# Audio tower on one core: tokens, attention and experts in one pass; two steps of the expert round, the emptying of a shared bank and the routing are put elsewhere in the order

## What is computed

```
h = tok(x)            # 3 patch sizes (8, 16, 32; stride half a patch): 127 + 63 + 31 = 221 tokens of 128
                      # each token = patch @ W_i.T + b_i + pos_i + scale_emb_i
h = h + attn(layernorm(h))     # 8 heads of 16, softmax over the 221 tokens, output matrix w_agg
h = h + ffn(layernorm(h))      # "batch" of 1024 tokens: 2 of 8 experts per token,
                               # y = gelu(z @ w1[e]) @ w2[e], added with the router weight
```

## Time and profile before

| what | value |
|---|---|
| runs, median | 309.08 us (306.54 to 309.54) |
| the profiled execution | 307.14 us |
| its span | 305.3 us |
| TensorE busy, share of the span | 269.8 us, 88% |
| VectorE busy | 199.5 us, 65% |
| ScalarE busy | 143.3 us, 47% |
| GpSimd busy | 109.4 us, 36% |
| TensorE's mean granted clock | 0.935 of full speed |

### The profile page before, as it was taken

One profiled execution on the slowest core, in us unless ns is written; L12 is line 12 of the kernel. 1 busy time (PEld: TensorE's weight loads), 2 busy tenths in 40 slices (PEclk: granted clock), 3 DMA queues, 4 the chain that ended last, 5 costly groups with the idle time before them and its releaser, 6 DMA issues.

```text
span 305.3 us, 7681 instructions
## 1 busy us (share of the span) xinstructions
PE 269.8 (88%) x3147; PEld 230.8 (76%) x3147; DVE 199.5 (65%) x440; ACT 143.3 (47%) x220; POOL 109.4 (36%) x172
## 2 busy tenths in 40 slices
PE   8999869889999999999979798998979797998461
PEld 8999859677879797979768696877868696877331
DVE  4786674787888678785745567574756656475654
ACT  4650414533434352525456557564666466565220
POOL 4000220102455555555614264543636272422200
PEclk9999988999999999999979889997999899899755
DMA  7999000394000000000210020111011010001241
GB/s 206 380 381 422 9 1 2 84 344 125 20 10 24 15 22 15 18 24 13 68 29 17 11 54 17 36 34 37 26 34 37 10 52 11 17 26 35 78 136 46
DMA packets 19466, 22.33 MB, mean 73 GB/s; under 512 B 2416, under 2 KB 15448, under 8 KB 19400
## 3 DMA queue, kind: packets, MB, share of 16 engines
q1 hardware_dynamic: 17671, 19.24, 20.1%
q0 software_dynamic: 1760, 2.60, 2.8%
HBM read 17.42 MB, written 5.95 MB: 77 GB/s over the span
## 4 chain that ended last, share of the span: by engine, by line
PE 69%; DVE 12%; issue 6%; ACT 6%; DMA 4%; POOL 1%; SPq 0%; DVEq 0%; POOLq 0%; ACTq 0%
PE e_ps L982 13%; PE s_ps L1065 12%; PE s_ps L982 7%; PE e_ps L1186 7%; DVE nmax L801 7%; PE m_ps L1050 5%; PE m_ps L1173 4%; PE m_ps L1131 4%; PE s_ps L1118 3%; PE e_ps L1173 2%; PE m_ps L1040 2%; PE m_ps L1142 2%; DMA x_raw<-x 2%; DMA y_rows<-y_sb,idx_u 2%; ACT hidT L588 1%
## 5 line engine op out<-in xcount | busy, mean ns | idle before, releaser
L801 DVE TENSOR_REDUCE nmax<-s_ps 128x4 fp32r<-128x884 f32 (+1 forms) x64 | 65.9, 1071 | 24.8 <-PE s_ps L1065 24.8
L573 ACT ACTIVATE probs<-s_ps 128x888 f32<-128x888 f32 (+1 forms) x64 | 54.7, 906 | 57.9 <-PE s_ps L1118 57.9
L473 POOL DMA_INDIRECT y_rows<-y_sb,idx_u x23 | 23.0, 999 | 62.5 <-PE s_ps L1118 40.2
L1131 PE MATMUL m_ps<-probs,v_aug 93*32 93x221 f32 (+1 forms) x512 | 28.8, 366 | 0.7 <-ACT probs L573 0.7
L454 POOL DMA_INDIRECT z_slots<-z,slot_u x20 | 22.6, 1128 | 16.4 <-PE s_ps L1118 11.8
L1050 PE MATMUL m_ps<-zT,wqkv_sb 128*128 128x221 f32 x64 | 17.3, 397 | 11.4 <-ACT h_sb L553 11.4
L426 POOL TENSOR_TENSOR var_eps<-mv,eps_t 128x2 f32<-128x2 f32 x16 | 3.2, 201 | 66.4 <-DVE mv L768 66.2
L1186 PE MATMUL e_ps<-w_now,hidT 128*128 128x128 f32 x184 | 25.3, 290 | 0.0
L786 DVE TENSOR_TENSOR k_lo<-m_ps,k_hi 128x442 fp32r<-128x442 f32 x16 | 9.9, 619 | 23.6 <-ACT k_hi L566 23.6
L1186 PEld LDWEIGHTS e_ps<-w_now,hidT 128*128 128x128 f32 x184 | 23.2, 203 | 1.3 <-issue 1.0
L1065 PE MATMUL s_ps<-k_hi,q_a 32*128 32x222 f32 (+1 forms) x256 | 18.5, 308 | 4.6 <-DVE nmax L801 3.3
(11 more groups left out here) (125 smaller groups left out, 619.6 us busy)
## 6 DMA issues: line engine op xcount, KB each, us to landing
w_raw<-wt SPq DMA_DIRECT2D x6, 512.0 KB, 9.5
x_raw<-x SPq DMA_DIRECT2D x6, 512.0 KB, 9.9
w_sb<-w SPq DMA_DIRECT2D x1, 2048.0 KB, 9.6
z_slots<-z SPq DMA_DIRECT2D x1, 1518.0 KB, 9.5
zs<-z_slots SPq DMA_DIRECT2D x7, 198.0 KB, 2.6
x_raw<-x SPq DMA_DIRECT2D x4, 256.0 KB, 5.1
out<-h SPq DMA_DIRECT2D x11, 64.0 KB
c_sb<-consts SPq DMA_DIRECT2D x1, 599.0 KB, 11.6
```

Source lines behind the costliest of these rows:

```text
L473: g.indirect_dma_start(y_dram, bass.IndirectOffsetOnAxis(ap=idx_u[:, at:at + 1], axis=0), y_sb[:, i, :], None).then_inc(y_out, 16)
L573: s.activation(probs[0:n, blk, 2 * f:2 * f + 2].rearrange("p t u n -> p t (u n)"), s_ps[0:n, 2 * f:2 * f + 2, 0:2 * NE], ACT.Exp, scale=DH ...
L801: v.tensor_reduce(nmax[0:n, blk, 2 * f:2 * f + 2, 0:2], src, AX_X, ALU.max, negate=True).then_inc(max_ready, 1)
L1131: mm = pe.matmul(bank[32 * t:32 * t + 32, :], v_aug[0:n, b % 2, blk, HALF * r + t, :], probs[0:n, blk, t, r, 0:N], start=(blk == 0), stop= ...
```

## The change

- **TensorE.** `project_k(c+1)` stands behind the first half of the second scores instead of behind `place_max`. `zs_turn(0)` stands ahead of `pv(6)` in cycle 7. `zs_turn(n)` for n > 0 waits for the Gelu of tile 1 of the round before (`e_ps` is what that tile used) instead of that round's last. `project_q(1)` waits for the copy of v of sequence 0.
- **ScalarE.** In the cycles with experts `h_copy(c+2)` is ahead of `q_high(c+1)`. In the others the order stays.
- **VectorE.** `hT_evac` of a unit that ended in the cycle before and `y_evac` stand ahead of `maxima(c,0)`. `zsT_evac(n+1)` stands ahead of `norm`. `route_slots` moves from the end of cycle 0 to ahead of `k_low(1)`; the copy of v of sequence 0 and `lo_x(7)` (the low part of a piece of x) go from the ends of cycles -1 and 0 to between the two maxima of cycle 0.
- **GpSimd.** h plus bias waits for the normalised z of the same sequence (`z_ready`) instead of for h itself.
- **The y buffer** is doubled, with a semaphore for each half, so that `y_evac` waits for the scatters of two rounds earlier.
- **PLAN.** Cycle 0 goes from (18, 10, 0, 14, 6) to (18, 8, 0, 10, 12), and cycles 1 to 6 from (0, 10, 0, 18, 20) to (4, 10, 0, 14, 20). The sums are the same (48).

```diff
--- before.py
+++ after.py
@@ -89,8 +89,8 @@
 UNIT_AT = {0: 0, 1: 127, 2: 190}
 
 
-PLAN = {-2: (0, 28, 0, 0, 0), -1: (4, 8, 0, 2, 6), 0: (18, 10, 0, 14, 6), 1: (0, 10, 0, 18, 20), 2: (0, 10, 0, 18, 20),
-        3: (0, 10, 0, 18, 20), 4: (0, 10, 0, 18, 20), 5: (0, 10, 0, 18, 20), 6: (0, 10, 0, 18, 20)}
+PLAN = {-2: (0, 28, 0, 0, 0), -1: (4, 8, 0, 2, 6), 0: (18, 8, 0, 10, 12), 1: (4, 10, 0, 14, 20), 2: (4, 10, 0, 14, 20),
+        3: (4, 10, 0, 14, 20), 4: (4, 10, 0, 14, 20), 5: (4, 10, 0, 14, 20), 6: (4, 10, 0, 14, 20)}
 
 
 
@@ -251,7 +251,7 @@
         hidT = sb("hidT", [P, ROUND, FC, P])
         zs = sb("zs", [P, ROUND, ROW])
         zsT = sb("zsT", [P, ROUND, P])
-        y_sb = sb("y_sb", [P, ROUND, P])
+        y_sb = sb("y_sb", [P, 2, ROUND, P])
         g_sb = sb("g_sb", [P, FJ, TOP_K, P])
 
         s_ps = ctx.enter_context(nc.psum_tensor("s_ps", [P, 4, 512], F32))
@@ -300,7 +300,8 @@
         scattered = [sem(f"scattered{i}") for i in range(2)]
         zs_in, zs_turned, zsT_ready = sem("zs_in"), sem("zs_turned"), sem("zsT_ready")
         w1_ready, w2_ready, hid_done, hidT_ready = sem("w1_ready"), sem("w2_ready"), sem("hid_done"), sem("hidT_ready")
-        y_done, y_ready, y_out = sem("y_done"), sem("y_ready"), sem("y_out")
+        y_done, y_ready = sem("y_done"), sem("y_ready")
+        y_out = [sem(f"y_out{i}") for i in range(2)]
         combined, final_out = sem("combined"), sem("final_out")
 
         block = ctx.enter_context(nc.Block())
@@ -364,7 +365,8 @@
                              ).then_inc(zs_in, 16)
 
             def load_y():
-                sp.wait_ge(y_out, 16 * N_TILES)
+                for i in range(2):
+                    sp.wait_ge(y_out[i], 16 * sum(ROUND_TILES[i::2]))
                 y = y_dram[0:T_FFN * TOP_K].rearrange("(n k) d -> n (k d)", k=TOP_K)
                 whole = (FFN_B - 1) * N
                 for t in range(2):
@@ -426,7 +428,7 @@
                 g.tensor_tensor(var_eps[:], mv[:, :, 1], eps_t[:], ALU.add).then_inc(eps_added, 1)
                 pool.wait_ge(eps_added, b + 1)
                 g.tensor_tensor(rstd[:], var_eps[:], mhalf_t[:], ALU.pow).then_inc(rstd_ready, 1)
-                pool.wait_ge(h_ready, b + 1)
+                pool.wait_ge(z_ready, b * 2 + 2)
                 if b > 3:
                     pool.wait_ge(h1_ready, b - 3)
                 g.tensor_tensor(hb[:, b % 4], h_sb[:], bagg_sb[:].unsqueeze(1).to_broadcast([P, 2, P]),
@@ -471,7 +473,7 @@
                     pool.wait_ge(idx_ready, n + 1)
                 at = TILES_BEFORE[n] + i
                 g.indirect_dma_start(y_dram, bass.IndirectOffsetOnAxis(ap=idx_u[:, at:at + 1], axis=0),
-                                     y_sb[:, i, :], None).then_inc(y_out, 16)
+                                     y_sb[:, n % 2, i, :], None).then_inc(y_out[n % 2], 16)
 
             def fetch_w1(n, lo, hi):
                 if not 0 <= n < ROUNDS:
@@ -642,9 +644,11 @@
                 gelu(n, 3)
                 if experts:
                     load_table(ACT.Exp)
+                if experts and c + 2 < BATCH:
+                    h_copy(c + 2)
                 if 0 <= c + 1 < BATCH:
                     q_high(c + 1)
-                if c + 2 < BATCH:
+                if not experts and c + 2 < BATCH:
                     h_copy(c + 2)
                 if c == -2:
                     hi_x(6)
@@ -874,9 +878,9 @@
                     return
                 m = ROUND_TILES[n]
                 dve.wait_ge(y_done, n + 1)
-                if n:
-                    dve.wait_ge(y_out, 16 * TILES_BEFORE[n])
-                v.tensor_copy(y_sb[:, 0:m, :].rearrange("p i d -> p (i d)"), e_ps[:, 0:m * P]).then_inc(y_ready, 1)
+                if n >= 2:
+                    dve.wait_ge(y_out[n % 2], 16 * sum(ROUND_TILES[n % 2:n:2]))
+                v.tensor_copy(y_sb[:, n % 2, 0:m, :].rearrange("p i d -> p (i d)"), e_ps[:, 0:m * P]).then_inc(y_ready, 1)
 
             lo_x(0)
             lo_w(0)
@@ -902,15 +906,18 @@
 
             for c in range(-2, BATCH + 1):
                 n = c - E0
+                if (c - 1, 1) in UNIT_ENDS:
+                    hT_evac(UNIT_ENDS[(c - 1, 1)])
+                y_evac(n - 1)
                 if 0 <= c < BATCH:
                     maxima(c, 0)
-                if (c - 1, 1) in UNIT_ENDS:
-                    hT_evac(UNIT_ENDS[(c - 1, 1)])
+                if c == 0:
+                    v_copy(0)
+                    lo_x(7)
                 if 0 <= c - 2 < FFN_B:
                     ffn_z(c - 2)
                 if n == 0:
                     zsT_evac(0)
-                y_evac(n - 1)
                 if 0 <= c < BATCH:
                     maxima(c, 1)
                 if c == BATCH:
@@ -921,14 +928,16 @@
                     nmaxT_copy(c)
                 if (c, 0) in UNIT_ENDS:
                     hT_evac(UNIT_ENDS[(c, 0)])
+                if n >= 0:
+                    zsT_evac(n + 1)
                 if c - 1 >= 0:
                     norm(c - 1)
-                if n >= 0:
-                    zsT_evac(n + 1)
                 if 0 <= c + 1 < BATCH:
                     q_low(c + 1)
                 if c + 2 < BATCH:
                     ln_stats(c + 2)
+                if c == 0:
+                    route_slots()
                 if 0 <= c + 1 < BATCH:
                     k_low(c + 1)
                 if c + 2 < BATCH:
@@ -936,11 +945,8 @@
                 if c == -2:
                     route_tiles()
                     lo_x(6)
-                if 0 <= c + 1 < BATCH:
+                if 0 < c + 1 < BATCH:
                     v_copy(c + 1)
-                if c == 0:
-                    lo_x(7)
-                    route_slots()
                 if c == 1:
                     lo_x(8)
                 if c == 2:
@@ -1036,6 +1042,8 @@
                 pe.wait_ge(zT_ready, b + 1)
                 if b >= 2:
                     pe.wait_ge(o_raw_ready, b - 1)
+                elif b == 1:
+                    pe.wait_ge(v_ready, 1)
                 for u in range(2):
                     mm = pe.matmul(m_ps[:, 0, u * N:(u + 1) * N], wqkv_sb[:, u, :], zT[:], start=True, stop=True)
                 mm.then_inc(q_done, 1)
@@ -1148,7 +1156,7 @@
                     return
                 pe.wait_ge(zs_in, 16 * (n + 1))
                 if n:
-                    pe.wait_ge(hidT_ready, TILES_BEFORE[n])
+                    pe.wait_ge(hidT_ready, TILES_BEFORE[n - 1] + 2)
                 else:
                     pe.wait_ge(hT_ready, len(UNITS))
                     pe.wait_ge(w2_in, 16)
@@ -1222,10 +1230,10 @@
                     z_turn(c + 1)
                 if n > 0:
                     hidden(n, 0)
+                if n == 0:
+                    zs_turn(0)
                 if behind:
                     pv(c - 1)
-                if n == 0:
-                    zs_turn(0)
                 tok_some(p1)
                 keep(k1, *free)
                 if here:
@@ -1243,14 +1251,14 @@
                 keep(k2, *free)
                 if here:
                     place_max(c)
-                if ahead1:
-                    project_k(c + 1)
                 if n >= 0:
                     zs_turn(n + 1)
                 tok_some(pm)
                 if here:
                     s2_products(c, 0)
                     s2_maxima(c, 0)
+                if ahead1:
+                    project_k(c + 1)
                 tok_some(p3)
                 keep(k3, *free)
                 down(n, 0, 2)
```

## The result

The changed kernel takes 281.16 us in the median of four runs (280.32 to 282.13); the kernel before, with one more run, 309.06 (306.54 to 309.54). The ratio is 0.911, 95% interval 0.905 to 0.917. The forecast was 284.0, range 279.5 to 292. The profiled execution of the changed kernel took 282.13 us, span 280.3, against 307.14 and 305.3. The ratios here, and the medians of the kernel before that the experiments are set against, leave out executions more than 1.5% over the fastest of the same kernel on the same chip.

The account below looks back on a forecast made before the run. TensorE, nearly full, was taken as the bound, losing time only in waits and at low clock. Terms 10.0 + 6.1 + 4.1 + 3.0 + 0.2 + 0 = 23.4 took 307.14 to 283.7, stated as 284.0 us; range 279.5 to 292.

Parts of the forecast that it names:

- The wait at `project_k`: Cycles 8 to 13: TensorE's wait for the copy of h goes, 1.64 us a cycle, 9.7 us in six waits.
- The clock: Cycles 8 to 13: time lost at 1.2 GHz behind gaps of 1.64 us all won back, 6.1 us; bounds 0 and 6.1.
- Rival 1: Expert cycles: the waits go but low-clock spells stay at some other place; 290.1 us, chance 0.15.
- rival 3: Cycles 7 to 13: the clock falls in a gapless TensorE, making the kernel slower, 312 us at clock 0.78; chance 0.03.
- Rival 2: The wait at `project_k` is half replaced, as `s2_maxima` waits for `nmaxT` or h is later; 291.9 us, chance 0.11.
- Cycle 0: `hT_evac` first lets the tokens start earlier without a gap, routing moves ahead of `k_low(1)`; 4.1 us saved.
- Cycles 1 to 6: Cycle 1's wait of 1.8 us for maxima goes, and 1.2 us in cycles 2 to 6; sum 3.0 us.
- the four tokens: Cycles 2 to 6: tokens between `pv` and `s1(c,1)` cover about 0.2 us of idle a cycle, 1.2 in all.
- Cycle 7: `zs_turn(0)` ahead of `pv(6)` loses 1.7 us against 1.64 won at `project_k`; sum 0, bounds -1.6 and +1.6.
- h plus bias: Ahead of cycle 0: GpSimd's addition waits for z, so two slow VectorE instructions leave TensorE's way; 0.2 us won.
- y_sb: One `hidden` waiting for `y_sb`: goes because the copy now waits for scatters of two rounds before; 0.3 us.
- the two ties: Two places where the new order is tight, `nmaxT` and h, under 0.1 us a cycle; 283.7 taken as 284.0.

Follow-up runs that it names:

- experiment 2: Kernel before with six float32 matmuls of zeros put ahead of `project_k` in cycles 7 to 13, all waits kept: 302.50 us, ratio 0.979.
- experiment 1: Kernel before with only `project_k` moved, h copied ahead of q in expert cycles, and `zs_turn` waiting for the Gelu of tile 1: 290.60 us, ratio 0.940.
- experiment 4: Changed kernel with q copied ahead of h again, `project_k` still in its new place: 286.81 us, ratio 0.930.
- experiment 9: Kernel before with `hT_evac` ahead of maxima, v copy, `lo_x(7)` and routing moved, `project_q(1)` waiting for the v copy, new PLAN: 299.90 us, ratio 0.986.
- experiment 3: Changed kernel with `project_k` back directly behind `place_max`, h still copied ahead of q: 292.62 us, ratio 0.948.
- experiment 11: Changed kernel with h plus bias waiting for h itself again: 282.59 us, ratio 0.928.
- experiment 12: Changed kernel with the old PLAN: 281.17 us, ratio 0.924.
- experiment 6: Changed kernel with `pv` back ahead of the first turn, `zs_turn(0)`, in cycle 7: 282.06 us, ratio 0.908.
- experiment 10: Changed kernel with one y buffer, `y_evac` still ahead of the maxima: 297.03 us, ratio 0.975.

## Why the prediction was right, point by point

- **The wait at `project_k`** went, in all seven cycles, and nothing took its place. Its size was low: 9.7 us forecast for cycles 8 to 13, 10.6 measured (experiment 2 against experiment 1). `down` moved up by 1.76 us, not 1.64, since the wait in the earlier trace rows is counted from the modelled end of a pipelined matmul (222.98 + 0.40) while the next instruction can start 0.24 behind its start (206.50 to 206.74). The remaining 0.1 a cycle lies behind `down`. What the forecast had as the next to be late, the exponentials, was not: they start 208.38 - 199.37 = 9.01 us into the cycle, before it was 227.27 - 215.85 = 11.42, so 2.4 us earlier where 2.3 was forecast.
- **The clock** came back whole: 6.1 forecast, 6.3 by experiment 2, 1.00 in the trace. Rival 1 (290.1) is out, and so is rival 3 (slower), as TensorE is 99.8% busy in cycles 8 to 13 at a clock of 1.00. The page "TensorE: Matmul & The Clock Gate" of the Trainium skill (Part 1, What's actually happening) puts the ramp penalty, for modelling, at under 1% of a typical kernel span. The trace disagrees as to size for this kernel, whose clock falls again and again: 6.3 us of 309 are 2.0%, in one stretch.
- **Rival 2** (half replaced, 291.9) did not come, but experiment 4 shows how near it was: 0.5 us of delay of h is 0.48 us a cycle.
- **Cycle 0**: 4.1 forecast, 4.06 measured, with the 0.36 us wait at `place_max` where it was foretold. That the two agree so closely is in part luck. The early edits alone gave 3.3 (experiment 9); the place of `project_k` gave 0.5 of it (experiment 3), which the prediction's sum for this cycle does not name, and h plus bias 0.3 (experiment 11), which it placed ahead of the cycle.
- **Cycles 1 to 6**: 3.0 forecast, 2.36 measured. The term mis-sized is the four tokens: 1.2 forecast for cycles 2 to 6, 0.75 measured, of which the PLAN is 0.5 (experiment 12). The forecast took the whole idle time as won and put nothing for taking four tokens out of their run, which cost 0.2 of each 0.26.
- **Cycle 7**: 0 forecast, 0.55 saved. The wait for the rows was 1.97, not 2.3, as they came 3.02 us into the cycle (141.46 - 138.44), where the turn had started at 3.26 before (148.56 - 145.30). The edit itself was a loss, as forecast (1.7; 1.5 by experiment 6), with 1.7 more behind it at the lower clock. Without it the cycle took 15.14 us, 3.8 less than before.
- **h plus bias**: 0.2 forecast, ahead of cycle 0; 0.3 measured in cycle 0. Its cause, the overlap with the addition, is seen in experiment 11. The 0.44 saved ahead of cycle 0 is not settled: cycle 0 begins at 40.17 to 40.95 us in the nine profiles with the edit and at 40.66 to 41.31 in the five without.
- **y_sb**: the wait of 0.3 is gone, as forecast, but not for the reason given. Experiments 1, 2 and 9 have one buffer and the old place of `y_evac`, and their profiles have no such wait either, so this term was right by luck. Experiment 10 adds that the second buffer carries some 15 us in the new order, which the prediction had not priced.
- The total of 281.16 is 2.8 under the forecast. The profile explains 1.6 of it: 25.0 us saved in place of 23.4, beside a median that is 1.0 below the profiled execution, and 0.3 that I had added for the two ties, which cost nothing. Not taken apart by any run are VectorE's new order in the expert cycles (`y_evac` and `zsT_evac`) and the turn's condition; with the other edits they share the 0.5 us of cycles 8 to 13 and the 10.6 of the expert edits.

## What to carry to other kernels

On an engine that is nearly full, look for what stands behind a wait and does not need it; moving the waiting instruction back in its list is worth the wait, and more if the gap left the clock low behind it (here 10.6 us and 6.3). Count the two apart by filling the gap with dummy matmuls: that kernel keeps the wait and gives back the clock. A small wait can be hardly worth filling: taking four matmuls out of a run cost 0.21 us here, of the 0.26 that they filled.

## What the runs showed that I had not expected

- Gaps of 1.1 us in each of cycles 8 to 13 left the clock at 1.00 (experiment 3, one profile), gaps of 1.6 lowered it in four of these six (in the kernel before and in experiment 9). But length alone did not decide: in experiment 10 it fell behind 1.69 us and not behind 2.86, and the wait of 1.8 to 2.0 in cycle 7 lowered it in four profiles of eight.
- ScalarE stood 4.2 to 5.2 us at the same instruction of cycle 6 in all eight profiles from two chips and in none of the six others, with nothing in the trace to release it. What it was stays open.
- Eighteen token matmuls cost 2.32 us behind one another (experiment 12) and 2.53 in two places.
- VectorE's z takes 0.344 us alone and 0.631 in the median beside an addition of GpSimd.
